# Grouping the U products in pairs, and issuing the repeats of each gated block from two queues

## The chip, the cores and the metric

The kernel runs on one core of a Trainium2 chip. The metric is the device time of one execution in microseconds, as the median of a few runs. The rows of the profile come from one further execution.

## What is computed

For 8 sequences of 1024 tokens with 512 channels in float32, two layers each add to their input. The first is an adapter with weights chosen by a language number. The second uses exponential moving averages over time:

```
x = x + layernorm(x + relu(x W1[lang] + b1) W2[lang] + b2) * gamma0 + beta0
ctx    = ema(x, tau_ctx)
gated  = x * sigmoid([x, ctx] Wg + bg)
mod    = 0.5 + sigmoid(gelu(x Wn1 + bn1) Wn2 + bn2)          # 8 values per token
traces = ema(gated * mod[d], tau[d])  for d = 0..7
temporal = sum over d of traces[d] * softmax(blend)[d]
gate   = sigmoid(temporal Wtemp + btemp)
soma   = gelu(x Wsoma + bsoma)
x = x + layernorm((soma * gate) Wout) * gamma1 + beta1
```

Here ema(b)[t] = alpha * ema(b)[t-1] + b[t].

## The kernel before

The 8192 tokens are cut into 16 tiles of 512, and each tile into 4 blocks of 128 tokens. A tile takes one slot, and the slots follow one another. Five programs run side by side, one for each engine: SyncE (SP) issues nearly all DMAs, ScalarE (ACT) does sigmoid, gelu and the rounded high parts, VectorE (DVE) does the elementwise work, GpSimd (POOL) does some additions, TensorE (PE) the matmuls. Each engine runs its instructions in the order written, and waits on semaphores where a `wait_ge` stands. The orders are written out by hand.

Large products are made of three matmuls each (high times high, high times low, low times high), all 128x128 weights with 512 columns. They write to five PSUM banks used in turn (`ring`), in the order that `groups_of` lists; before a bank is written again PE waits for its reader (`free_bank`).

The part that the change touches is how the eight traces of a block are made. Block b of the gated values, `g[:, b, :]`, is opened by ACT (`open_gate(b)`, a sigmoid), multiplied by DVE (`gated(b)`), and stored by ACT to memory (`store_spans(b)`, 256 KB). It is then read back four times over: `repeat_spans(b)` issues NQ = 4 DMAs of 256 KB, number q of which fills partitions 32q to 32q+31 of a buffer with the whole block, cut in four spans of 32 tokens. Blocks 0 and 2 land in `grep[0]`, block 1 in `grep[1]`, block 3 in the tile's `x1` buffer. All repeats are issued by SP, which waits first for the landing of the store (`g_stored[b]`), then for the buffer to be free.

DVE multiplies a landed block with the blend weights: `products(b, hh, c)` makes one piece of `U` (128x1024), for two halves of the traces (hh) and two halves of the channels (c), four pieces a block. There are four buffers for pieces of U. PE turns each pair of pieces into part of the trace with `within_spans(b, hh)`: matmuls with weights 128x32 and 256 columns that write 32 partitions each. A call of it is 16 matmuls in the profile, 8 for each piece (each float32 matmul appears twice). `from_before(b)` adds what came before the block (3 matmuls, with V, the states of the spans), ACT copies the bank (`trace(b)`), and `trace_by_channels(b)` transposes it for the next tile's gate.

V comes about thus: PE's `span_states()` needs all four gated blocks, DVE scales the result (`span_states()`, L878), ACT rounds it (`states_high()`, L538), DVE takes the low part (`states_low()`, L884). In DVE's order `states_low()` stands between `products(1, 1, 0)` and `products(1, 1, 1)`; `gated(3)` stands ahead of `products(1, 0, 0)`. In ACT's order, ahead of the soma and trace work of the slot:

```
store_spans(0)
for b in range(1, NB):
    open_gate(b)
    store_spans(b)
states_high()
```

Between the `within_spans` PE does the soma products, 12 matmuls each, split in two halves of six (`soma_begun(e)`, `soma_ended(e)`). In tiles with an even number there is also `tile_state()`, three matmuls. After the repeats of a tile SP issues the store of the next tile's x1 and the loads for the tile after it.

Of the kernel before, what the change touches and what calls it, by code (L numbers as in the profile page):

```python
# [11 lines left out]
NB = TOK // P  # L12
NC = C // P
L = 32
NI = P // L
NQ = 4
# [24 lines left out]
def cond_resid_kernel(nc, x, xc, ids, w1, w2, b1, b2, g0, be0, wg, wn1, wsoma, wtemp, wout, wn2,  # L41
# [10 lines left out]
    with ctx:  # L52
# [164 lines left out]
        def upto(per_tile, tile, j):  # L217

            return tile * per_tile + (j + 1)
# [63 lines left out]
        def _(sp):  # L283
# [56 lines left out]
            def slot(k):  # L340
                has_prev, has_cur, has_next = parts_of(k)

                def repeat_spans(b):


                    sp.wait_ge(g_stored[b], 16 * upto(1, k, 0))
                    if b == 2:
                        sp.wait_ge(U_ready, upto(PIECES, k, 3))
                    elif b == 3:
                        sp.wait_ge(g_ready, upto(4, k, b))  # L350
                        sp.wait_ge(x1_stored, 16 * upto(1, k, 0))
                    elif b == 0 and has_next:
                        sp.wait_ge(x1_ready, upto(4, k + 1, NB - 1))
                    for q in range(NQ):
                        sp.dma_start(spans_of(k, b)[q * L:(q + 1) * L, :, :],  # L355
                                     g_dram[b].rearrange("(i s) c -> s i c", i=NI)).then_inc(spans_in(k, b)[0], 16)

                if has_prev:
                    if has_next:
                        if k & 1:  # L360
                            load_language((k + 1) // 2)
                        sp.wait_ge(U_ready, upto(PIECES, k - 1, PIECES // 2 - 1))
                        load_xT(k + 1)
                        sp.wait_ge(U_ready, upto(PIECES, k - 1, 3 * PIECES // 4 - 1))
                        load_x(k + 1)
                        sp.wait_ge(full["h"], upto(1, k + 1, 0))
                    else:
                        sp.wait_ge(U_ready, upto(PIECES, k - 1, PIECES // 2 - 1))
                    sp.dma_start(x1_back[:, :, :].rearrange("p b c -> p (b c)"), x1_dram[(k - 1) & 1]).then_inc(ld_back, 16)
                    for b in range(NB):  # L370
                        sp.wait_ge(res_ready, upto(4, k - 1, b))
                        sp.dma_start(out_tiles[k - 1, b * P:(b + 1) * P, :], res[:, b, :]).then_inc(stored, 16)
                else:
                    second_loads()
                if has_cur:
                    for b in range(NB):
                        repeat_spans(b)
                if has_next:
                    sp.wait_ge(x1_stored, 16 * upto(1, k, 0))
                    keep_x1(k + 1)  # L380
# [71 lines left out]
        def _(act):  # L452
# [6 lines left out]
            def slot(k):  # L459
# [67 lines left out]
                def store_spans(b):  # L527
                    act.wait_ge(g_ready, upto(4, k, b))
                    nc.scalar.dma_start(g_dram[b], g[:, b, :]).then_inc(g_stored[b], 16)

                def open_gate(b):
                    act.wait_ge(pre_ready, upto(4, k, b))
                    nc.scalar.activation(g[:, b, :], g[:, b, :], ACT.Sigmoid).then_inc(sig_ready, 1)  # L533

                def states_high():
                    rows = state_rows(k)
                    act.wait_ge(V_ready, upto(1, k, 0))
                    nc.scalar.activation(V_hi[rows, :], smp[rows, :], ACT.Identity).then_inc(Vhi_ready, 1)  # L538
# [5 lines left out]
                if has_cur:  # L544
                    if k == 0:
                        split(4)
                        split(5)
                    open_gate(0)
                    act.wait_ge(m_pre, upto(1, k, 0))
                    nc.scalar.activation(m_nat, m_nat, ACT.Sigmoid).then_inc(msig_ready, 1)  # L550
                    if k == 0:
                        act.wait_ge(tables_ready, 1)
                        nc.scalar.activation(Epow[0][:, :, :], Epow_raw[:, :, :], ACT.Identity).then_inc(tablehi_ready, 1)
                        nc.scalar.activation(Eend[0][:, :], Eend_raw[:, :], ACT.Identity).then_inc(tablehi_ready, 1)
                    store_spans(0)
                    for b in range(1, NB):
                        open_gate(b)
                        store_spans(b)
                    states_high()
                    soma_gelu(1)  # L560
                    trace(0)
                    trace(1)
                    trace_high(0)
                    soma_gelu(2)
                    trace(2)
                    trace_high(1)
                    trace(3)
                    trace_high(2)
                    if not k & 1:

                        act.wait_ge(full["carry"], k // 2 + 1)
                        nc.scalar.activation(V_hi[96:128, :], smp[96:128, :], ACT.Identity).then_inc(carry_ready, 1)
                    if has_next:
                        soma_gelu(3)
                        trace_high(3)
                    else:
                        trace_high(3)
                        soma_gelu(3)
# [394 lines left out]
        def _(pe):  # L973
# [14 lines left out]
            def slot(k):  # L988
# [37 lines left out]
                def soma_begun(e):  # L1026

                    ps = free_bank(pe, "soma", k, e)
                    at = slice(e * P, (e + 1) * P)
                    split_product(ps[:, :], lambda a, n: Wsoma[a][:, n, at], lambda a, n: x1T[a][:, n, :],  # L1030
                                  NC // 2, final=False)

                def soma_ended(e):

                    at = slice(e * P, (e + 1) * P)
                    split_product(bank_of("soma", k, e)[:, :], lambda a, n: Wsoma[a][:, n, at], lambda a, n: x1T[a][:, n, :],
                                  NC, begin=NC // 2, first=False).then_inc(full["soma"], 1)
# [60 lines left out]
                def value_gate(b):  # L1098

                    ps = free_bank(pe, "wg", k, b)  # L1100
                    at = slice(b * P, (b + 1) * P)
                    split_product(ps[:, :], lambda a, n: x1T[a][:, n, at], lambda a, n: Wg[a][:, n, :], NC, final=False)
                    if b == 0:
                        pe.wait_ge(emalo_ready, upto(4, k, NC - 1))
                        if k == 0:
                            pe.wait_ge(split_lo[3], 1)
                    split_product(ps[:, :], lambda a, n: seq[a][:, n, at], lambda a, n: Wg[a][:, NC + n, :], NC,
                                  first=False).then_inc(full["wg"], 1)
# [77 lines left out]
                if has_cur:  # L1186
                    if k == 0:
                        pe.wait_ge(split_lo[1], 1)
                    soma_of(0)
                    if k == 0:  # L1190
                        pe.wait_ge(split_lo[2], 1)
                    value_gate(0)
                    modulation()
                    value_gate(1)
                    spread_modulation()
                    value_gate(2)
                    value_gate(3)
                    within_spans(0, 0)
                    soma_begun(1)
                    within_spans(0, 1)  # L1200
                    span_states()
                    soma_ended(1)
                    within_spans(1, 0)
                    soma_begun(2)
                    from_before(0)
                    within_spans(1, 1)
                    from_before(1)
                    within_spans(2, 0)
                    trace_by_channels(0)
                    soma_ended(2)  # L1210
                    within_spans(2, 1)
                    from_before(2)
                    soma_begun(3)
                    within_spans(3, 0)
                    trace_by_channels(1)
                    if not odd:
                        tile_state()
                    within_spans(3, 1)
                    from_before(3)
                    trace_by_channels(2)  # L1220
                    if has_next:
                        soma_ended(3)
                        trace_by_channels(3)
                    else:
                        trace_by_channels(3)
                        soma_ended(3)
# [86 lines left out]
```

## Time and profile before

| | |
|---|---|
| three runs | 1365.42, 1373.02, 1372.81 us; median 1372.81 us |
| profiled execution, its own time | 1370.63 us |
| its span, first to last instruction | 1368.8 us |
| mean granted TensorE clock | 0.993 of full speed |
| PE busy | 1326.8 us, 97% of the span |
| DVE, ACT, POOL busy | 1032.8, 522.2, 373.9 us |
| DMA | 186.25 MB, mean 136 GB/s |
| a tile in the steady state | about 82.4 us |

The profiled execution lies 2.2 us under the median of the runs. A busy PE in this profile means that a matmul was in the pipeline, and successive matmuls overlap: a 128x512 matmul lasts 0.39 us and the next one starts 0.23 us after it. What a stretch of PE work costs is therefore read from the starts of the matmuls, not from their durations.

### The profile page before, as it was taken

Reading aid. Unit: us, or ns where it says so; the run is one execution under the profiler, and the core shown is the slowest. Engines: PE = TensorE matmul, PEld = TensorE weight load, DVE = VectorE, ACT = ScalarE, POOL = GpSimd, SP = SyncE. Lnnn points to the kernel's source line nnn. Section 1 sums busy time; section 2 is a strip of 40 time slices with the busy share of each in tenths; the row PEclk is TensorE's granted clock in tenths of the full one; section 3 lists DMA queues with packets and bytes.
Section 4 is the critical chain, followed back from the end, with each engine's and each line's share of the span. In section 5 each row is a group of like instructions: output and inputs, shape, how many; then the busy total and the mean of one; then the engine's idle time right before and its main releaser. Section 6 shows DMA issues by size and latency. Waiting matters only on the chain.

```text
span 1368.8 us, 19735 instructions
## 1 busy us (share of the span) xinstructions
PE 1326.8 (97%) x7908; PEld 982.6 (72%) x7908; DVE 1032.8 (75%) x1526; ACT 522.2 (38%) x822; POOL 373.9 (27%) x294
## 2 busy tenths in 40 slices
PE   4789999999999999999999999999999999999997
PEld 2657768677786767868677686767868677786766
DVE  6997777786778777687786778877777787778575
ACT  3425244252533425244242433425244252433422
POOL 3406123041420504124041322314123041321102
PEclk9899999999999999999999999999999999999999
DMA  7373451916328082461806627074451825426070
GB/s 265 123 205 111 120 180 60 227 69 171 137 85 231 35 227 78 115 204 66 238 32 158 188 78 201 31 215 131 112 166 70 218 90 154 154 77 170 27 190 31
DMA packets 91486, 186.25 MB, mean 136 GB/s; under 512 B 9858, under 2 KB 14594, under 8 KB 87298
## 3 DMA queue, kind: packets, MB, share of 16 engines
q1 hardware_dynamic: 82178, 168.20, 41.8%
q10 hardware_dynamic: 9216, 16.78, 3.7%
q8 instruction: 63, 1.03, 0.3%
q14 instruction: 29, 0.24, 0.1%
HBM read 134.61 MB, written 50.33 MB: 135 GB/s over the span
## 4 chain that ended last, share of the span: by engine, by line
PE 73%; DVE 9%; DMA 6%; issue 5%; ACT 2%; SPq 1%; POOL 1%; DVEq 0%; POOLq 0%
PE ring L984 51%; PE Tp L1158 7%; PE ring L977 4%; PE Tp L1169 3%; DMA grep<-g_blocks 3%; DMA g_blocks<-g_f 3%; PE ring L1183 2%; DVE U L863 2%; PE Tp L984 2%; SPq L355 1%; DVE x L793 1%; PE ring L1004 1%; PE Tp L1004 1%; DVE stats L798 1%; ACT U L523 1%
## 5 line engine op out<-in xcount | busy, mean ns | idle before, releaser
L863 DVE TENSOR_TENSOR U<-grep,w_qs 128x1024 f32<-128x1024 f32 x192 | 227.3, 1218 | 52.9 <-issue 36.1
L412 POOL TENSOR_TENSOR x<-grep,b_row 128x512 f32<-128x512 f32 x64 | 80.0, 1283 | 543.2 <-DMA grep<-in_x 543.2
L1158 PE MATMUL Tp<-U,Arep 128*32 128x256 f32 x2048 | 139.5, 386 | 3.4 <-DVE U L863 3.1
L533 ACT ACTIVATE g_f<-g_f 128x512 f32<-128x512 f32 x64 | 40.4, 632 | 258.2 <-DVE g_f L868 258.1
L425 POOL TENSOR_TENSOR grep<-grep,beta_row 128x512 f32<-128x512 f32 x64 | 82.7, 1326 | 125.3 <-DMA grep<-x_tiles 125.2
L984 PE MATMUL ring<-x1T_hi,Wsoma_hi 128*128 128x512 f32 x256 | 108.3, 423 | 0.0
L868 DVE TENSOR_TENSOR g_f<-ring,bg_row 128x512 f32<-128x512 f32 x64 | 44.1, 689 | 84.8 <-PE ring L984 84.6
L984 PE MATMUL ring<-seq_hi,Wtemp_hi 128*128 128x512 f32 x256 | 106.6, 417 | 0.1
L1158 PEld LDWEIGHTS Tp<-U,Arep 128*32 128x32 f32 x2048 | 51.9, 109 | 74.2 <-issue 38.8
L984 PE MATMUL ring<-Wg_hi,x1T_hi 128*128 128x512 f32 x256 | 103.2, 403 | 0.0
L984 PE MATMUL ring<-Wout_hi,g_r 128*128 128x512 f32 x256 | 99.8, 390 | 1.1 <-DVE soma_r L720 1.0
L984 PE MATMUL ring<-x1T_hi,Wsoma_r 128*128 128x512 f32 x256 | 100.5, 393 | 0.0
L984 PE MATMUL ring<-x1T_lo,Wsoma_hi 128*128 128x512 f32 x256 | 100.1, 391 | 0.0
L984 PE MATMUL ring<-Wg_hi,x1T_lo 128*128 128x512 f32 x256 | 100.1, 391 | 0.0
L984 PE MATMUL ring<-Wg_r,x1T_hi 128*128 128x512 f32 x256 | 99.8, 390 | 0.0
L984 PE MATMUL ring<-seq_hi,Wtemp_r 128*128 128x512 f32 x256 | 99.8, 390 | 0.0
L984 PE MATMUL ring<-seq_lo,Wtemp_hi 128*128 128x512 f32 x256 | 99.7, 390 | 0.0
L984 PE MATMUL ring<-Wout_r,g_r 128*128 128x512 f32 x256 | 99.6, 389 | 0.0
L984 PE MATMUL ring<-Wout_hi,soma_r 128*128 128x512 f32 x256 | 99.6, 389 | 0.0
L984 PE MATMUL ring<-Wg_hi,seq_hi 128*128 128x512 f32 x256 | 99.6, 389 | 0.0
L984 PE MATMUL ring<-Wg_r,seq_hi 128*128 128x512 f32 x256 | 99.6, 389 | 0.0
L984 PE MATMUL ring<-Wg_hi,seq_lo 128*128 128x512 f32 x256 | 99.6, 389 | 0.0
(173 smaller groups left out, 2884.0 us busy)
## 6 DMA issues: line engine op xcount, KB each, us to landing
grep<-g_blocks SPq DMA_DIRECT2D x192, 256.0 KB, 4.5
grep<-in_xc SPq DMA_DIRECT2D x16, 1024.0 KB, 11.3
grep<-in_x SPq DMA_DIRECT2D x16, 1024.0 KB, 9.0
x_tiles<-x SPq DMA_DIRECT2D x16, 1024.0 KB, 9.0
g_blocks<-g_f ACTq DMA_DIRECT2D x64, 256.0 KB, 3.7
x<-g_blocks SPq DMA_DIRECT2D x64, 256.0 KB, 5.7
grep<-x_tiles SPq DMA_DIRECT2D x16, 1024.0 KB, 4.8
out<-U SPq DMA_DIRECT2D x64, 256.0 KB, 2.0
```

What stands on the lines that cost most here:

```text
L355: sp.dma_start(spans_of(k, b)[q * L:(q + 1) * L, :, :], g_dram[b].rearrange("(i s) c -> s i c", i=NI)).then_inc(spans_in(k, b)[0], 16)
L412: nc.gpsimd.tensor_tensor(new[:, b, :], x_t[:, b, :], b2_row[:, :], ALU.add).then_inc(xb2_ready, 1)
L425: nc.gpsimd.tensor_tensor(x1_back[:, b, :], x1_back[:, b, :], beta1_row[:, :], ALU.add).then_inc(x1b_ready, 1)
L533: nc.scalar.activation(g[:, b, :], g[:, b, :], ACT.Sigmoid).then_inc(sig_ready, 1)
L863: V_.tensor_tensor(U[:, (n + 2) % 4, :, :], spans_of(k, b)[:, :, at], w_qs[:, hh, at].unsqueeze(1).to_broadcast([P, NI, HC]), ALU.mult).th ...
L868: V_.tensor_tensor(g[:, b, :], bank_of("wg", k, b)[:, :], bg_row[:, :], ALU.add).then_inc(pre_ready, 1)
L977: last = nc.tensor.matmul(dst, lhsT(n), rhs(n), start=(n == 0), stop=(n == steps - 1))
L984: last = nc.tensor.matmul(dst, lhsT(a, n), rhs(b, n), start=(first and n == begin and m == 0), stop=(final and n == steps - 1 and m == 2))
L1004: last = nc.tensor.transpose(ps[:, b * P:(b + 1) * P], x1[odd ^ 1][:, b, n * P:(n + 1) * P], ident[:, :])
L1158: last = nc.tensor.matmul(Tp[b % 2][i * L:(i + 1) * L, at], Arep[:, b * NI + i, hh, :], U[:, (n + 2) % 4, i, :], start=(hh == 0 and c == 0 ...
L1169: last = nc.tensor.matmul(Tp[b % 2][:, :], Epow[a][rows, b, :], V[c][rows, :], start=False, stop=(m == 2))
L1183: last = nc.tensor.transpose(ps[:, n * P:(n + 1) * P], T_sb[b % 2][:, n * P:(n + 1) * P], ident[:, :])
```

## The change

Two things change. First, SP issues only the repeats with q = 0 and 1 of each block, and ACT issues those with q = 2 and 3, right behind the store of the block, with a wait for the landing of that store and the same waits for a free buffer. Second, PE's order is changed so that the two `within_spans` of a block follow one another, with the soma products moved out from between them.

```
@@ SP
-                    for q in range(NQ):
+                    for q in range(NQ // 2):
@@ ACT
+                def repeat_spans(b):
+                    act.wait_ge(g_stored[b], 16 * upto(1, k, 0))
+                    if b == 0 and has_next:
+                        act.wait_ge(x1_ready, upto(4, k + 1, NB - 1))
+                    elif b == 1 and has_prev:
+                        act.wait_ge(res_ready, upto(4, k - 1, NB - 1))
+                    elif b == 2:
+                        act.wait_ge(U_ready, upto(PIECES, k, 3))
+                    elif b == 3:
+                        act.wait_ge(x1_stored, 16 * upto(1, k, 0))
+                    for q in range(NQ // 2, NQ):
+                        nc.scalar.dma_start(spans_of(k, b)[q * L:(q + 1) * L, :, :],
+                                            g_dram[b].rearrange("(i s) c -> s i c", i=NI)).then_inc(spans_in(k, b)[0], 16)
...
                     store_spans(0)
+                    repeat_spans(0)
                     for b in range(1, NB):
                         open_gate(b)
                         store_spans(b)
+                        repeat_spans(b)
                     states_high()
@@ PE
+                    soma_begun(1)
                     within_spans(0, 0)
-                    soma_begun(1)
                     within_spans(0, 1)
                     span_states()
                     soma_ended(1)
+                    soma_begun(2)
                     within_spans(1, 0)
-                    soma_begun(2)
+                    within_spans(1, 1)
                     from_before(0)
-                    within_spans(1, 1)
                     from_before(1)
+                    soma_ended(2)
+                    trace_by_channels(0)
                     within_spans(2, 0)
-                    trace_by_channels(0)
-                    soma_ended(2)
                     within_spans(2, 1)
                     from_before(2)
                     soma_begun(3)
+                    trace_by_channels(1)
                     within_spans(3, 0)
-                    trace_by_channels(1)
+                    within_spans(3, 1)
+                    from_before(3)
                     if not odd:
                         tile_state()
-                    within_spans(3, 1)
-                    from_before(3)
                     trace_by_channels(2)
```

## Rows read from the trace of the kernel before

**Rows 1.** The page, part 1: busy time, share of the span, instructions.
```profile
PE 1326.8 (97%) x7908; PEld 982.6 (72%) x7908; DVE 1032.8 (75%) x1526; ACT 522.2 (38%) x822; POOL 373.9 (27%) x294
```

**Rows 2.** Waits of the span: total us, times, longest us.
```profile
DVE U L863 <- DMA grep<-g_blocks: 16.7, 15, 1.8
```

**Rows 3.** Chain that ended last, one odd tile: start us, us, what.
```profile
482.14 2.61 DMA g_blocks<-g_f
...
484.76 0.33 SPq L355
...
494.71 3.99 DMA g_blocks<-g_f
...
498.72 0.30 SPq L355
...
500.02 6.68 DMA grep<-g_blocks
```

**Rows 4.** Timeline of ACT, the same tile: start us, us, what, [idle before].
```profile
487.56 0.33 ACTq L529 DMA_DIRECT2D g_blocks<-g_f  x1
...
497.64 0.63 ACT L533 ACTIVATE g_f<-g_f 128x512 f32<-128x512 f32 x1 [4.03 <-DVE g_f L868]
499.03 0.36 ACTq L529 DMA_DIRECT2D g_blocks<-g_f  x1
502.14 0.60 ACT L538 ACTIVATE V_hi_r<-smp 120x512 fp32r<-120x512 f32 x1 [3.87 <-DVE smp L878]
```

**Rows 5.** Stores issued at 487.56 and 577.70: KB, us to landing.
```profile
g_blocks<-g_f ACTq DMA_DIRECT2D x1, 256.0 KB, 4.0
...
g_blocks<-g_f ACTq DMA_DIRECT2D x1, 256.0 KB, 3.8
```

**Rows 6.** Timeline of DVE, the same odd tile.
```profile
498.31 0.69 DVE L872 TENSOR_TENSOR g_f<-g_f,x 128x512 f32<-128x512 f32 x1 [0.70 <-ACT g_f L533]
...
503.15 0.68 DVE L884 TENSOR_TENSOR V_lo_r<-smp,V_hi_r 120x512 fp32r<-120x512 f32 x1
503.75 1.22 DVE L863 TENSOR_TENSOR U<-grep,w_qs 128x1024 f32<-128x1024 f32 x1
506.73 4.63 DVE L863 TENSOR_TENSOR U<-grep,w_qs 128x1024 f32<-128x1024 f32 x4 [1.76 <-DMA grep<-g_blocks]
```

**Rows 7.** Timeline of PE, the same odd tile.
```profile
505.59 0.39 PE L1169 MATMUL Tp<-V_lo_r,Epow_hi 128*128 128x512 f32 x1
505.82 0.40 PE L1169 MATMUL Tp<-V_hi_r,Epow_r 128*128 128x512 f32 x1
506.14 1.07 PE L1158 MATMUL Tp<-U,Arep 128*32 128x256 f32 x16
507.14 0.50 PE L1169 MATMUL Tp<-V_hi_r,Epow_hi 128*128 128x512 f32 x1
...
508.10 0.64 PE L1158 MATMUL Tp<-U,Arep 128*32 128x256 f32 x8
...
517.54 0.50 PE L1169 MATMUL Tp<-V_hi_r,Epow_hi 128*128 128x512 f32 x1
...
518.36 0.60 PE L1183 MATMUL ring<-ident,T_sb_f 128*128 128x128 f32 x4
518.71 0.48 PE L984 MATMUL ring<-x1T_hi,Wsoma_hi 128*128 128x512 f32 x1
```

**Rows 8.** Timelines of ACT and of PE in the next tile, an even one.
```profile
577.70 0.33 ACTq L529 DMA_DIRECT2D g_blocks<-g_f  x1
...
598.32 0.47 PE L1176 MATMUL smp<-V_hi_r,Eend_hi 128*128 128x512 f32 x1
...
600.19 0.50 PE L1169 MATMUL Tp<-V_hi_r,Epow_hi 120*128 120x512 f32 x1
```

**Rows 9.** DMA rate in 40 slices of 491.5 to 498.8, and of 511 to 523.
```profile
GB/s 0 0 0 0 0 79 146 11 180 325 449 359 292 224 213 191 213 202 213 157 258 348 269 225 225 202 224 202 213 202 213 213 247 314 314 202 56 0 0 0
...
GB/s 437 410 369 348 403 396 416 403 403 416 410 314 396 416 382 403 396 410 396 430 266 157 34 0 0 0 0 0 0 0 0 0 0 0 0 0 0 0 0 0
```

## The prediction

> **What bounds the kernel now.** I read the page first. PE is busy 97% of the span [rows 1], so a gain has to come either from PE work made cheaper or from the few places where PE waits. Next I read the waits. DVE waits once per tile, about 1.1 us, for the repeats of block 2 (16.7 us over 15 tiles) [rows 2]. The chain of waits over one odd tile shows why: a store of a gated block lands about 4 us after its issue, SP then issues four repeats, and the last of them lands at 506.70 [rows 3]. Last I read the timelines of DVE, PE and ACT for that tile [rows 4, 6, 7]. DVE begins block 2 at 506.73, the moment the repeat is there, and PE's last groups of the tile follow DVE's pieces closely. So in this stage PE's own work, DVE's pieces and the repeats are all nearly critical, and a delay of over a microsecond in any of them reaches the end. The rest of the slot (gates, output, soma) is dense PE work. Therefore I measure a tile by one mark, the start of `from_before(3)`, which is 517.54 in the odd tile and 600.19 in the next, even one [rows 7, 8]. What follows the mark stays the same but for one step, counted below.
>
> **Part 1, the pairing on PE.** A lone `within_spans` starts 0.32 after the matmul before it, where a 128x128 one starts 0.23 after: 0.09 more. The next wide matmul starts 1.00 after the group's start, and the one after that later than usual by 0.13, since three matmuls and their successor take 0.82 where 0.23 each would give 0.69 [rows 7]. One piece alone lasts 0.64 and two last 1.07, so a piece adds 0.43, and a second group behind the first should cost 0.86 instead of 1.00 [rows 7]. I take the same cadence of 0.43 across the border of the groups, which no row shows; the lone price is its upper bound. A pairing then saves 0.09 + 0.13 + 0.14 = 0.36 us, four of them in 16 tiles 23 us. This is a gain only if PE is what decides. Moving `tile_state` behind the mark adds three matmuls there in even tiles, 3 x 0.23 = 0.7 us.
>
> **Part 2, two repeats leave SP.** SP's four issues begin 1.30 apart from first to last, 0.43 each [rows 3]. With two per queue the last begins 0.35 to 0.45 after the first. At most 0.95 us is saved on each block, at least nothing, because the transfer itself is the longer piece: after a short burst the rate stays at 190 to 230 GB/s for the whole of a block's repeats, while the loads to 128 partitions run at about 400 [rows 9]. I take 0.2 us per block, near the lower end, since four requests already queue behind each other. SP itself gains 0.9 us per block, worth nothing: nobody waits for what follows.
>
> **Part 3, ACT now waits.** This is the part that decides. ACT runs in order, and its new wait for the landing of store b stands ahead of `open_gate(b+1)` and, for b = 3, ahead of `states_high()`. Blocks 0 and 1 do no harm: store 0 lands at 484.75 [rows 3], ACT has issued its pair at 485.6, and with a sigmoid and a product still between, store 1 left only at 487.56 [rows 4]. Followed through the odd tile:
> - Store 2 is issued at 494.71 and lands at 498.7 [rows 3]. Two issues take 0.8, so ACT is free at 499.5. Its sigmoid of block 3 started at 497.64 [rows 4]; it is 1.9 late.
> - From that sigmoid to DVE's `gated(3)` is 0.67, from there to store 3 is 0.72 [rows 4, 6]: store 3 goes out at 500.9, not 499.03. DVE stands still meanwhile, as `products(1, 0, 0)` is behind `gated(3)`, and PE's `span_states` stands too.
> - Store 3 lands in the traffic of block 2's repeats, begun at 498.7. The nearest case is store 1, issued 2.8 after block 0's repeats began (484.76) and landed 4.0 later, 6.8 after their begin [rows 3 to 5]. I take 6.8: 505.5. The bounds are 3.8 after its issue, 504.7 [rows 5], and the end of block 2's traffic as it was, 8.0 after its begin, 506.7 [rows 3].
> - ACT issues its pair (0.8) and only then rounds V (0.6), 506.9 instead of 502.7. DVE's `states_low` takes 0.6 and `products(1, 1, 1)` 1.2 [rows 4, 6]: its piece is ready at 508.7 instead of 504.97, 3.7 us late.
> - PE reaches this piece at about 506, so it waits. Block 2 has landed by then, so the old wait of DVE is gone. From here on, with t the time of that piece: half a group 0.57, twelve matmuls 0.82 + 9 x 0.23 = 2.9, four transposes 0.35 and the entry 0.09 give t + 3.9 for block 2's groups; 1.86 for the pair, nine matmuls 2.2, transposes and entry 0.44 give t + 8.4 for block 3's; its last piece is reached at t + 9.7. DVE needs 4.63 + 0.6 + 4.63 = 9.9 for the eight pieces and one low part [rows 6], so PE gets it at t + 9.8, and the mark is at t + 10.4 [rows 7].
>
> **The sum.** Odd tile: 508.7 + 10.4 = 519.1 against 517.54, 1.6 us late. Even tile: store 2 goes out at 577.70 and lands 3.8 later, 581.5 [rows 5, 8]; store 3 goes out at 583.7 and lands at 588.3; the piece is ready at 591.5, the mark at 601.9 against 600.19: 1.7 us, and 0.7 for `tile_state`. The mean is 2.0 us. The drains of blocks 1 and 2 both lie on this path, so 0.2 us saved on each takes off 0.4, leaving 1.6 us a tile and 26 us for 16 tiles. Against the profiled execution's own 1370.6 us this is 1397; the median of the runs stands 2.2 us above, so I predict **1399 us**. With the bounds of the landing (-0.8 and +1.2 a tile) the case spans 1386 to 1418.
>
> The Trainium skill, "DMA: Bandwidth & Descriptors", section "Issuing engines are not separate DMA queues", says that DMAs begun on several engines run on the same sixteen engines and save only the sequencer's time. By that rule the sum stays at 26 to 32 us, less at most the issue time bounded above.
>
> **Rival A, two queues fill two halves at once: faster.** SP now fills partitions 0 to 63 and ACT 64 to 127 together, where one queue filled them in turn. For it: 200 GB/s against 400 for full-width loads, and a bump to 348 GB/s in the middle of block 1's repeats, where the third repeat takes over from the second [rows 9]. Against it: both queues feed the same engines, and the burst at the start appears with a single queue too. At 400 GB/s 1 MB takes 2.6 us instead of 5.1. Then block 1 is in before store 2 goes out, and store 2 lands in 2.6 as store 0 did [rows 3], at 497.3; store 3 goes out at 499.5 and lands after some 3.2 (between 2.6 and 3.8), 502.7; the piece is ready at 505.9, the mark at 516.3. That is 1.2 us earlier in odd tiles, 0.4 in even ones (1.1 less 0.7), 13 us in all: 1360 us. It decides once the two drains together are more than 2.0 us shorter, 1.0 of 6.8 us each.
>
> The skill's "SBUF — State Buffer", section "Door 1: The DMA port swizzle", puts partitions 0 to 63 on one half of the ports and 64 to 127 on the other, which is this rival's mechanism. The same page reports that two concurrent transfers to the two halves gained only 6%, which speaks for the forecast; no run so far shows either.
>
> **Rival B, the two effects cancel.** The drains get about 1.0 us shorter each, by part overlap plus the issue time. The delay of 2.0 us a tile is then paid back: 1373 us.
>
> **Rival C, the pairing pays in full.** ACT's waits hide and PE alone decides: 23 us less, 1350 us. Against it: the piece behind `states_low` cannot come before ACT has issued its second pair.
>
> **Chances.** Forecast 0.55, rival A 0.22, rival B 0.18, rival C 0.05. Differences under 1% cannot be told from none here, so faster means under 1359 and slower above 1387. A sits on the first border, so I give half of it and all of C to faster, and a little more: 0.18. B, the rest of A and the forecast's low tail make 0.29 for same, and 0.53 is left for slower. The range reaches from below A, 1354, to 1412 within the forecast's upper tail.
>
> **What would show it.** Right: ACT's sigmoid of block 3 near 2 us later than before, measured from the last gate product; `states_high` 4 us later; a new wait of PE for U in the second group of block 1; no wait of DVE for block 2's repeat; the DMA rate still near 200 GB/s. Wrong: the rate near 400 during the repeats, stores landing in under 3 us, or the mark earlier than before. The pairs themselves are right if two groups start 0.86 apart.

## The result and the profile after

| kernel | median us | lowest, highest | profiled execution, its span | mean granted clock |
|---|---|---|---|---|
| before | 1372.91 | 1365.42, 1373.9 | 1370.63, 1368.8 | 0.993 |
| after | 1399.59 | 1395.73, 1406.9 | 1406.9, 1405.1 | 0.984 |

The change makes the kernel slower: ratio 1.0207, 95% interval 1.0172 to 1.0241. The profiled execution of the changed kernel is the slowest of its four, 7.3 us above the median. So its trace shows some 36 us of loss where the median shows 27. One execution of experiment 1's kernel below, 2846.97 us at full clock, is left out of its ratio as slow.

The page of the kernel after, part 1, and its views of waits (total us, times, longest us). They answer to [rows 1, 2].

```profile
PE 1326.9 (94%) x7908; PEld 1004.1 (71%) x7908; DVE 1036.7 (74%) x1526; ACT 521.2 (37%) x822; POOL 375.2 (27%) x294
...
ACT V_hi_r L552 <- DMA g_blocks<-g_f: 88.8, 15, 7.1
...
PEld Tp L1174 <- DVE U L879: 50.8, 36, 3.7
...
ACT g_f L547 <- DMA g_blocks<-g_f: 41.7, 7, 6.2
...
DVE V_lo_r L900 <- ACT V_hi_r L552: 27.5, 16, 3.0
```

PE has the same work as before (1326.9 us busy), in a longer span. DVE's wait for the repeats of block 2 is gone. In its place ACT waits for the landing of its own stores, ahead of V's rounding and ahead of the sigmoid; DVE waits for the rounded V; PE waits for DVE's pieces, its weight loads up to 3.7 us at once and its matmuls up to 3.2.

The chain of waits through the same odd tile as in [rows 3], start us, us, what:

```profile
502.09 3.46 DMA g_blocks<-g_f
505.55 0.02 issue
505.57 0.36 ACTq L542
505.93 0.03 issue
505.96 0.46 ACTq L542
506.42 0.05 issue
506.46 0.64 ACT g_f L547
...
507.12 0.70 DVE g_f L888
...
507.85 5.41 DMA g_blocks<-g_f
...
514.16 0.61 ACT V_hi_r L552
...
515.39 1.23 DVE U L879
516.62 0.04 issue
516.66 1.08 PE Tp L1174 x8
```

This is the forecast's path, link by link: store 2, ACT's two issues, the late sigmoid of block 3, store 3, ACT's two issues, the rounding of V, the piece behind `states_low`, and PE. Before the change the chain of this stretch ran over SP and the repeats instead. PE in the same tile; these rows answer to [rows 7]:

```profile
506.28 1.93 PE L1174 MATMUL Tp<-U,Arep 128*32 128x256 f32 x32
508.03 1.04 PE L1156 MATMUL smp<-g_f,Bm 128*32 128x512 f32 x8
...
511.95 1.50 PE L1174 MATMUL Tp<-U,Arep 128*32 128x256 f32 x24
516.66 1.08 PE L1174 MATMUL Tp<-U,Arep 128*32 128x256 f32 x8 [3.21 <-DVE U L879]
...
518.27 0.63 PE L1185 MATMUL Tp<-V_lo_r,Epow_hi 128*128 128x512 f32 x1
518.69 0.63 PE L1185 MATMUL Tp<-V_hi_r,Epow_r 128*128 128x512 f32 x1
...
528.59 0.50 PE L1185 MATMUL Tp<-V_hi_r,Epow_hi 128*128 128x512 f32 x1
```

Three things are to be seen. The pair takes 508.03 - 506.28 = 1.75 us up to the next group, so the pairing works as costed. PE stands 3.21 us for the last piece of block 1. And behind that wait the same matmuls are slow: a piece takes 1.08 instead of 0.64, and matmuls follow each other in 0.42 instead of 0.23. The reason is the clock. The rows below are stretches of 1 us of this tile. The columns are the length, the busy us of PE, PE's weight loads, DVE, ACT and POOL with their instructions, the granted clock, the DMA share and GB/s:

```profile
513.00:514.00 1.00, 0.45 (x11) 0.00 (x0) 0.00 (x0) 0.00 (x0) 0.00 (x0) 1.00 0.00 0
514.00:515.00 1.00, 0.00 (x0) 0.00 (x0) 0.21 (x1) 0.82 (x2) 0.00 (x0) 1.00 0.90 100
515.00:516.00 1.00, 0.00 (x0) 0.00 (x0) 1.00 (x2) 1.00 (x1) 0.00 (x0) 1.00 0.49 176
516.00:517.00 1.00, 0.34 (x4) 0.20 (x8) 1.00 (x2) 0.74 (x2) 0.00 (x0) 0.64 1.04 330
517.00:518.00 1.00, 1.00 (x9) 0.33 (x2) 1.00 (x2) 0.00 (x0) 0.00 (x0) 0.50 1.06 254
518.00:519.00 1.00, 1.00 (x3) 0.81 (x3) 1.00 (x2) 0.00 (x0) 0.00 (x0) 0.50 1.10 361
519.00:520.00 1.00, 1.00 (x4) 0.76 (x4) 1.00 (x2) 0.60 (x1) 0.00 (x0) 0.66 1.01 426
520.00:521.00 1.00, 1.00 (x6) 0.79 (x5) 1.00 (x2) 0.60 (x1) 0.00 (x0) 1.00 0.99 418
```

Near the end of PE's standstill of 3.2 us the granted clock falls from 1.00 to 0.50, the lower level of 1.2 GHz, and it comes back near 519.7. The piece and the six matmuls behind it take 3.4 us from start to start; at full clock they take 0.57 + 0.34 + 5 x 0.23 = 2.1.

The length of a wait alone does not tell whether the clock falls, and a fall can begin after PE has resumed. After the first 100 us the changed kernel's PE waits more than 1.5 us at fifteen places, and at eight of them the clock falls. The waits at these eight last 1.57 to 3.21 us, those at the other seven 1.57 to 1.97. In experiment 2 below, three waits of 2.4 to 2.5 us pass with the clock at 1.00. One place of each kind, first of the kernel after, then of experiment 2's (PE with its wait, then a stretch of 2 us behind it, columns as above):

```profile
180.35 0.64 PE L1174 MATMUL Tp<-U,Arep 128*32 128x256 f32 x8 [1.86 <-DVE U L879]
```

```profile
182.00:184.00 2.00, 2.00 (x6) 1.52 (x6) 2.00 (x3) 1.11 (x2) 0.00 (x0) 0.50 1.06 407
```

```profile
264.88 0.64 PE L1160 MATMUL Tp<-U,Arep 128*32 128x256 f32 x8 [2.43 <-DVE U L865]
```

```profile
264.00:266.00 2.00, 1.12 (x10) 0.64 (x11) 2.00 (x3) 0.95 (x2) 0.00 (x0) 1.00 1.02 264
```

To compare kernels I use two numbers. The first is the mean over 16 tiles of the forecast's mark: the start of `from_before(3)`, counted from the start of the last `value_gate` matmul of the tile. The second is the clock loss: (1 - granted clock) times length, summed over stretches of 2 us from 100 us on, without the last microseconds of the span, where the clock falls in every kernel. It is an upper figure, as some of that time PE is idle anyway. For before they are 21.20 and 0.0 us, for after 22.89 and 15.4 us. Their first tiles aside, the marks of the changed kernel spread from 20.2 to 25.7 us, those of before from 20.4 to 21.6.

### The profile page after: what moved, and what is told of

It reads as the page before. It is cut to its first block, busy times and chain, and to the rows that moved or that the text cites. A ratio compares the mean times of both kernels' runs of the same rounds, so it can differ in the third digit from the quotient of the medians.

```text
span 1405.1 us, 19797 instructions
## 1 busy us (share of the span) xinstructions
PE 1326.9 (94%) x7908; PEld 1004.1 (71%) x7908; DVE 1036.7 (74%) x1526; ACT 521.2 (37%) x822; POOL 375.2 (27%) x294
## 4 chain that ended last, share of the span: by engine, by line
PE 65%; DVE 12%; DMA 10%; issue 4%; ACT 3%; ACTq 2%; POOL 1%; DVEq 0%; POOLq 0%
PE ring L1000 45%; DMA g_blocks<-g_f 9%; PE Tp L1174 5%; PE Tp L1185 4%; DVE U L879 4%; PE ring L993 3%; PE Tp L1000 2%; PE ring L1199 2%; ACTq L542 2%; DVE g_f L888 2%; DMA grep<-g_blocks 1%; PE Tp L1020 1%; PE ring L1020 1%; ACT g_f L547 1%; DVE g_f L884 1%
## 5 line engine op out<-in xcount | busy, mean ns | idle before, releaser
L1174 PE MATMUL Tp<-U,Arep 128*32 128x256 f32 x2048 | 131.3, 386 | 34.3 <-DVE U L879 34.3
L425 POOL TENSOR_TENSOR grep<-grep,beta_row 128x512 f32<-128x512 f32 x64 | 87.0, 1391 | 146.1 <-DMA grep<-x_tiles 146.1
L1174 PEld LDWEIGHTS Tp<-U,Arep 128*32 128x32 f32 x2048 | 56.4, 109 | 94.3 <-DVE U L879 50.8
```

The source lines that it names most:

```text
L425: nc.gpsimd.tensor_tensor(x1_back[:, b, :], x1_back[:, b, :], beta1_row[:, :], ALU.add).then_inc(x1b_ready, 1)
L1174: last = nc.tensor.matmul(Tp[b % 2][i * L:(i + 1) * L, at], Arep[:, b * NI + i, hh, :], U[:, (n + 2) % 4, i, :], start=(hh == 0 and c == 0 ...
```

## The experiments

All ratios are against the kernel before, timed on the same chip. The experiments were timed on three chips, on which the kernel before took 1371.5 to 1372.5 us; the changed kernel was timed beside one of 1372.9 us. So differences in microseconds between kernels are good to a few us only. "Paired" means PE's new order.

**1. The pairing alone (pair_only).** The changed kernel's PE order, with SP and ACT as before. Seen from the changed kernel:

```
-                    for q in range(NQ // 2):
+                    for q in range(NQ):
-                        repeat_spans(b)          # and repeat_spans(0), on ACT
```

> PE's new order alone; SP issues all four repeats as before and ACT waits for nothing new. Theory (ACT's in-order wait for the landing of its stores is what costs): DVE keeps its old pace, the mark of a tile moves 0.5 us forward at most and tile_state takes 0.7 us back in even tiles, so 0 to 8 us faster than before, ratio 0.994 to 1.000. Rival (the pairing itself costs, as PE meets U pieces too early and then stands): at least 15 us slower, ratio 1.01 or more.

Measured: 1361.71 us, ratio 0.9933 (0.9907 to 0.996). Mean mark 20.56, clock loss 3.4 us. The rival falls: the pairing pays, a bit more than the theory gave it. Full payment would have been 23 us. DVE's pieces most likely take the rest, as PE still waits for them (profile of this kernel, waits):

```profile
PEld Tp L1158 <- DVE U L863: 37.1, 56, 2.1
DVE U L863 <- DMA grep<-g_blocks: 12.7, 13, 2.6
```

**2. ACT's waits alone (wait_only).** As 1, and ACT waits where the change waits, but issues no repeats:

```
                     store_spans(0)
+                    act.wait_ge(g_stored[0], 16 * upto(1, k, 0))
                     for b in range(1, NB):
                         open_gate(b)
                         store_spans(b)
+                        act.wait_ge(g_stored[b], 16 * upto(1, k, 0))
```

> PE's new order, SP issues all four repeats, ACT issues none but waits for the landing of each store at the place where the change waits. Theory: the wait alone brings the loss back, ACT being 0.8 us freer per block but the transfer longer: ratio 1.010 to 1.025, PE waiting for U in the second group of block 1. Rival (not the wait but two queues sharing the DMA engines cost): same as the pairing alone, ratio within 0.003 of it.

Measured: 1415.18 us, ratio 1.0341 (1.0273 to 1.0409). Against experiment 1 the waits alone cost 53 us, 3.3 us a tile. The direction is the theory's, the size was outside its range. Mean mark 23.62, clock loss 17.1 us. No DMA was moved, so the two queues are not the culprit. Since the changed kernel has the same waits, and its two issues of 0.4 us behind each of them besides, and is still 16 us faster, its split must even help.

**3. The split with ACT's waits, PE in its old order (split_only).** The changed kernel with the PE order of before.

> The repeats from two queues with ACT's waits, PE in its old order. Theory: the late piece behind states_low is as late as in the changed kernel, and PE then takes the lone groups, each 0.36 us dearer: ratio 1.020 to 1.030. Rival (the pairing costs): ratio below 1.005, since two queues land a block about 0.8 us sooner.

Measured: 1386.24 us, ratio 1.0135 (1.0079 to 1.0192). Slower as the theory said, but less than it said: the new PE order does not soften the loss. By the medians it adds to it, though the two intervals overlap slightly (up to 1.0192 here, from 1.0172 in the changed kernel). The clock loss is 0.0 us here.

**4. ACT's waits with the old PE order (wait_old).** The kernel before with only the two `wait_ge` of experiment 2. It asks by a second pair of kernels what the pairing costs when a piece is late.

> The kernel before, with only ACT's waits for the landing of each store added; PE in its old order, all repeats from SP. Theory (with a late piece the pairing collects PE's idle time in one place, and costs instead of paying): PE still does from_before(0) in the shadow of the late piece and its gaps stay under 2 us, ratio 1.015 to 1.026, well under the 1.034 of the same waits with the pairing. Rival (pairing saves its 0.36 us per block whatever the rest does): ratio 1.040 or more.

Measured: 1397.23 us, ratio 1.0191 (1.0144 to 1.0237), as the theory said; the rival falls. With the same waits the pairing costs 18 us more (1415.18), and without them it saves 10. Clock loss 0.0 here, 17.1 with the pairing; the mean granted clock is 0.992 against 0.980. PE's waits behind the late V in this kernel:

```profile
PEld Tp L1171 <- DVE V_lo_r L886: 24.3, 15, 2.2
PE Tp L1171 <- DVE V_lo_r L886: 19.0, 15, 1.7
PEld Tp L1160 <- DVE U L865: 16.4, 42, 1.5
```

They are cut in two: first for V's low part ahead of `from_before(0)`, then for U, with work between. In the paired order the two fall into one (waits of wait_only):

```profile
PEld Tp L1160 <- DVE U L865: 55.7, 35, 3.8
PE Tp L1160 <- DVE U L865: 39.7, 21, 3.3
```

**5. Work moved into the gap (filled).** The changed kernel with one move on PE:

```
                     soma_begun(2)
+                    soma_begun(3)
                     within_spans(1, 0)
                     within_spans(1, 1)
...
                     from_before(2)
-                    soma_begun(3)
```

> The changed kernel with soma_begun(3) moved ahead of within_spans(1, 0), so that 1.4 us of work that PE does later stand in front of its long wait. The late piece comes no sooner. Theory (part of the loss is the granted clock, which falls to half after PE's gap of 3 us and more in some tiles): the gap shrinks by 1.4 us, the clock stays up, and PE catches up with DVE's pieces: 8 to 18 us faster than the changed kernel, ratio 1.008 to 1.015. Rival (only DVE's pieces decide behind the wait): within 4 us of the changed kernel, ratio 1.018 to 1.024.

Measured: 1390.44 us, ratio 1.0159 (1.0111 to 1.0208). That is 9 us under the changed kernel's median, just outside the ratio that the theory named, and its interval overlaps the changed kernel's. The time alone does not settle it. In the trace the clock loss falls from 15.4 to 5.1 us, and in the tile looked at PE waits 1.63 us and then runs a piece in 0.64 (PE of this kernel, [idle before]):

```profile
508.31 0.64 PE L1174 MATMUL Tp<-U,Arep 128*32 128x256 f32 x8 [1.63 <-DVE U L879]
508.88 0.50 PE L1185 MATMUL Tp<-V_hi_r,Epow_hi 128*128 128x512 f32 x1
509.22 0.39 PE L1185 MATMUL Tp<-V_lo_r,Epow_hi 128*128 128x512 f32 x1
```

Nor does this run part the clock from a plainer cause: the move also fills 1.4 us in which PE would have stood still, and that could shorten the tile by itself. By the ratios the gain is 7 us.

**6. Both of ACT's harmful waits moved back (split_late).** The changed kernel, in ACT's order (written here several calls to a line):

```
-                    for b in range(1, NB):       # open_gate(b), store_spans(b), repeat_spans(b)
+                    open_gate(1); store_spans(1); repeat_spans(1)
+                    open_gate(2); store_spans(2)
+                    open_gate(3); repeat_spans(2)
+                    store_spans(3)
                     states_high()
+                    repeat_spans(3)
```

> As the changed kernel, but ACT begins its repeats of block 2 behind the sigmoid of block 3, and those of block 3 behind states_high; PE's new order and both queues stay. Theory: ACT's waits now stand behind what others need, and block 2 lands 0.8 us sooner than before: ratio 0.985 to 0.997. Rival (the two queues or the pairing cost): stays at 1.015 or more.

Measured: 1359.68 us, ratio 0.9913 (0.9887 to 0.994), within the theory's range. Mean mark 20.16, clock loss 0.0. Both parts of the change are still in it, so neither the split nor the pairing is what costs; the place of ACT's waits is.

**7. Only block 3's pair behind the rounding of V (late_states).** The changed kernel with `repeat_spans(3)` moved behind `states_high()`.

> The changed kernel with one move: ACT's repeats of block 3 stand behind states_high. Theory: V is rounded at once and the piece behind states_low is held back only by the late gate of block 3, 1.9 us; about 2 us a tile come back: ratio 0.995 to 1.005. Rival (the late gate of block 3 is what decides, and V is only late because of it): no more than 0.5 us a tile comes back, ratio 1.015 or more.

Measured: 1365.31 us, ratio 0.9946 (0.9927 to 0.9965), just under the theory's range. One instruction group moved past another gives back 34 us of the changed kernel's median. Mean mark 20.38, clock loss 0.0.

**8. Only block 2's pair behind the sigmoid of block 3 (late_gate).** The changed kernel with `open_gate(3)` ahead of `repeat_spans(2)`; block 3's pair stays ahead of `states_high()`.

> The changed kernel with the other move: ACT's repeats of block 2 stand behind the sigmoid of block 3, those of block 3 still ahead of states_high. Theory: store 3 leaves about 1 us sooner, V is still held back until it lands: about 1 us a tile comes back, ratio 1.005 to 1.014. Rival (the late gate decides): near the pairing alone, 0.993 to 1.000.

Measured: 1418.14 us, ratio 1.0327 (1.0294 to 1.0359). A miss: not a microsecond came back, 19 us were lost. The chain of this kernel, same columns as above:

```profile
512.67 0.64 ACT g_f L547
...
513.33 0.70 DVE g_f L893
...
514.05 5.29 DMA g_blocks<-g_f
...
520.24 0.60 ACT V_hi_r L552
```

The sigmoid is on time, but store 3, now issued amid block 2's repeats, takes longer to land: 5.4 us in the median of the tiles against 4.1 in the changed kernel. What ends V's wait is the drain of the traffic around the store, not the moment of its issue. The traces show it over all 16 tiles (medians): store 3 leaves 1.1 us after block 2's first repeat here and 2.3 us after it in the changed kernel, block 2 takes 5.9 us from first issue to last landing in both, and in both store 3 lands 0.5 us after the last of these repeats. So V is rounded 8.8 us after the last `value_gate` matmul here and 8.9 us there: the earlier store bought nothing. The 19 us have another source. PE gets to its wait sooner, as the gate is on time, and stands there longer: its matmuls wait 47.5 us in all for pieces of U against 34.3, and the clock loss is 28.8 us, the largest of the study, against 15.4. That the clock makes up most of the 19 us fits these numbers, but no run tested it by itself.

**9. Both queues on the same half (same_half).** The changed kernel with SP issuing q = 0, 2 and ACT q = 1, 3:

```
-                    for q in range(NQ // 2):             # SP
+                    for q in (0, 2):
-                    for q in range(NQ // 2, NQ):         # ACT
+                    for q in (1, 3):
```

> The changed kernel, but SP issues the repeats 0 and 2 and ACT 1 and 3, so that both queues fill partitions 0 to 63 first and 64 to 127 then. Theory A (the higher rate in the changed kernel's repeats comes from filling both halves of the partitions at once): the rate falls back to about 200 to 230 GB/s, a block lands about 0.8 us later, and the kernel is 0.5 to 1% slower than the changed one, ratio 1.026 to 1.036. Rival (two queues do it, whatever they fill): like the changed kernel, ratio 1.017 to 1.024.

Measured: 1448.54 us, ratio 1.054 (1.0501 to 1.0579). Theory A's direction, over three times its size. Mean mark 25.70, clock loss 27.3 us. The same queues, bytes and waits; only which partitions are filled together differs. DMA rates in 40 slices while block 0 is repeated, first the kernel after (492.8 to 498.6), then this one (508.4 to 515.2):

```profile
GB/s 0 0 0 0 0 0 0 56 28 113 155 282 367 381 410 410 410 410 382 424 353 282 240 282 226 212 240 226 381 325 424 339 226 226 282 339 381 184 42 0
```

```profile
GB/s 0 0 0 0 0 12 108 108 96 217 289 386 410 361 253 229 217 193 205 205 193 217 229 325 217 205 217 241 217 217 205 205 193 205 193 253 361 349 145 36
```

After: over a microsecond at 350 to 424 GB/s, and a second, shorter rise. Same half: a short burst that reaches 410 as well, then about 205, which is the picture of before [rows 9]. From the first issue of block 0's repeats to DVE's first product of it this tile takes 6.4 us before (484.76 to 491.12), 5.6 after and 6.7 here. Over all tiles, the median from the first issue of a block's repeats to the last landing, blocks 0 to 3, is 6.6, 6.5, 7.1 and 7.8 us before, 5.5, 6.2, 5.9 and 6.4 after, and 6.6, 6.9, 6.6 and 7.2 here. Per DMA, from issue to landing (part 6 of the pages, after and then same_half):

```profile
grep<-g_blocks SPq DMA_DIRECT2D x96, 256.0 KB, 4.1
grep<-g_blocks ACTq DMA_DIRECT2D x96, 256.0 KB, 4.7
```

```profile
grep<-g_blocks SPq DMA_DIRECT2D x96, 256.0 KB, 4.8
grep<-g_blocks ACTq DMA_DIRECT2D x96, 256.0 KB, 5.6
```

**10. One queue, the halves in turn (pair_alternate).** As 1, all repeats from SP:

```
-                    for q in range(NQ):
+                    for q in (0, 2, 1, 3):
```

> The pairing alone, all four repeats from SP, in the order 0, 2, 1, 3 instead of 0, 1, 2, 3. Theory A (halves of the partitions decide): three borders between halves instead of one, a block lands 0.2 to 0.5 us sooner, ratio 0.988 to 0.993. Rival (one queue is worked off in order and gains nothing): equal to the pairing alone, 0.993, with the same time to landing.

Measured: 1358.0 us, ratio 0.9883 (0.9847 to 0.992). The interval overlaps that of experiment 1 a little, but the traces side with theory A: the median landing of a repeat to `grep` falls by 0.5 us (part 6 of the pages, experiment 1 and then this kernel),

```profile
grep<-g_blocks SPq DMA_DIRECT2D x192, 256.0 KB, 4.5
```

```profile
grep<-g_blocks SPq DMA_DIRECT2D x192, 256.0 KB, 4.0
```

and DVE's wait for repeats from 12.7 us to 2.6. From first issue to last landing block 0 takes 6.2 us instead of 6.5 (medians), within the 0.2 to 0.5 us of the theory. The rate no longer settles at 205; 40 slices of 481.4 to 487.4, block 0 of this kernel:

```profile
GB/s 0 0 0 0 0 0 96 177 191 164 287 369 355 287 314 341 410 287 301 219 232 218 341 314 164 164 177 300 287 410 342 300 246 219 314 423 232 218 41 0
```

Mean mark 19.96. This is the lowest median of the study, 1.1% under the kernel before and 41 us under the changed one, with no second queue at all. Its interval overlaps that of experiment 6.

**11. The same order of repeats in the kernel before (old_alternate).**

> The kernel before with one edit: SP issues the repeats in the order 0, 2, 1, 3. Theory (PE's lone groups are the floor in the old order, DVE only just behind them): marks fall to the 20.4 us that the best tiles of the old order have, 0.6 us a tile, ratio 0.992 to 0.996. Rival (the transfer of block 2 decides the old order's tiles): 1 us a tile or more, ratio 0.988 or less.

Measured: 1369.47 us, ratio 0.9982 (0.996 to 1.0004). No change that can be told, though DVE's wait for repeats to `grep` fell from 16.7 to 2.7 us. Without the pairing PE's lone groups are the floor, and quicker repeats have little to give. That was the theory's reason, but its size was too hopeful: its floor of 20.4 us left out `tile_state()`. The marks are now 20.39 us in most odd tiles and 21.08 in most even ones, which have these three matmuls ahead of the mark, so the mean fell only from 21.20 to 21.04.

The ratios side by side:

| how the repeats are begun | PE's old order | paired |
|---|---|---|
| SP, in order | 1 | 0.9933 |
| SP, ACT only waits | 1.0191 | 1.0341 |
| SP and ACT, as the change has it | 1.0135 | 1.0207 |
| SP, halves in turn | 0.9982 | 0.9883 |
| SP and ACT, ACT's waits moved back | not run | 0.9913 |

## Why the prediction was right, and where it was right by luck

The direction and its cause are shown. ACT's in-order wait costs 53 us by itself (experiment 2 against 1) and moving it gives the loss back (6 and 7). The predicted 1399 us and the measured 1399.6 agree better than the terms deserve: the loss from pairing and ACT's part was put at less than half, the gain from the filling of both halves at an eighth, and the clock was missing. Here is each step, by the tile that the forecast followed, from the start of its last `value_gate` matmul (496.49 before, 504.60 after):

- *The pairing.* Predicted 0.86 us for the second group; 1.75 us for two up to the next group against 0.89 for one gives 0.86. Right. As a saving it was worth 10 us alone, not 23, most likely because DVE's pieces follow closely: PE still waits for them in experiment 1.
- *The late sigmoid of block 3.* Predicted 1.9 us late; it starts at +1.86 instead of +1.15, so 0.7. Too large. Store 2 left 0.7 earlier and landed in 3.46 instead of 3.99 us, most likely because the repeats of blocks 0 and 1 landed sooner.
- *The landing of store 3.* Predicted 6.8 us after block 2's repeats began; 7.7 here (505.57 to 513.26), inside the bounds. The median of the tiles is 6.4.
- *The rounding of V and the piece.* Predicted 4.2 and 3.7 us late; +9.56 against +5.65 is 3.9, and the piece, ready at 516.6, is 3.5 late. Right in size, as the two errors before it cancel.
- *From the piece to the mark.* Predicted 10.4 us, measured 528.59 - 516.62 = 12.0. This is the missing term: the granted clock at 0.50 for about 3 us, which makes 1.3 to 1.4 of the 1.6 us (3.4 instead of 2.1 from the piece through six matmuls). The forecast had PE waiting some 2.7 us there and never asked what a stand of that length does to the clock.
- *What the split saves.* Predicted 0.2 us per block; 0.8 us on block 0 of this tile (6.4 to 5.6), and 1.1, 0.3, 1.2 and 1.4 us for blocks 0 to 3 by the medians of experiment 9. Some of the gain of blocks 2 and 3 is not the split's: with ACT's waits alone (experiment 2) block 2 already takes 6.5 us. Mis-sized: the forecast took the number nearest to "bound by the transfer", and gave the filling of both halves only a rival's chance. That rival's mechanism is real, in part.

By medians of whole kernels the pairing gave -10 us (1371.5 to 1361.7), ACT's waits +53 (to 1415.2) and the split -16 (to 1399.6). That is +28 against the kernel before of those runs, and +27 against the 1372.9 beside which the changed kernel was timed. These steps do not match the forecast's terms one for one. Its +32 us for pairing and ACT's part contain ACT's two issues of 0.8 us ahead of the sigmoid and ahead of the rounding, 1.6 us a tile or 26 us, which experiment 2 does not have.

The kernel that has all that the +32 us stand for, with transfers as slow as the forecast took them, is experiment 9. There block 0 takes 6.6 us to land, as before, and the kernel is 76 us slower (1448.5 against 1372.5). V is rounded 5.5 us later than before on the mean of the tiles, where the forecast followed 4.2, the mark comes 4.5 us later, and up to 27 us of the loss is clock. From there to the changed kernel the filling of both halves takes 49 us off, where the forecast had -6 for the split. So +32 stood for up to +76 and -6 for up to -49, and that the total came out at 26 against 27 is luck. How much of the 76 us belongs to two queues working on one half, a case that the forecast did not have, is open; block 1 takes 6.9 us there against 6.5 before.

Of the signs that the prediction named, four of the right ones came: `states_high` 3.9 us later in this tile, PE's new wait for U in block 1, no wait of DVE for block 2's repeat, and two groups 0.86 apart. Two did not: the sigmoid was 0.7 us late instead of near 2, and the rate did not stay near 200 GB/s. Two of the signs of being wrong came as well: rates near 400 during the repeats, and a store landing in under 3 us (block 1's, median 2.7). They belong to the misjudged split.

On rival A: its mechanism is shown by experiments 9 and 10, which change nothing but which partitions are filled together. Its sum failed because the drains of blocks 1 and 2 would have had to be 1.0 us shorter each, and they were 0.3 and 1.2 us shorter (medians), and because it too left out the clock. The Trainium skill, "SBUF — State Buffer", section "Door 1: The DMA port swizzle", puts partitions 0 to 63 and 64 to 127 on different ports; the order of the rates here agrees (same half about 205 GB/s after the burst, both halves 350 to 424 for over a microsecond). The same page, section "Can I just issue two DMAs to hit both halves?", reports only 6% for two concurrent transfers to the two halves. Here the block came 0.8 of 6.4 us sooner, over 12%, of which up to 0.95 us could also be issue time; but experiment 10, with one queue and the same number of issues, also shortened the landing by 0.5 of 4.5 us, and that cannot be issue time. On this the measurement decides, for this pattern of 2 KB runs to 32 partitions.

Rival B's amount did not come about, rival C's neither: its reason to fail, the piece behind `states_low`, is what the chain shows.

Still open: why the marks of the changed kernel scatter from 20.2 to 25.7 us from tile to tile, what decides which of PE's waits the clock falls at, and how much of the summed clock loss lay on the path.

## What to carry to other kernels

Before a DMA is moved to a compute engine's queue, write down what stands behind it in that engine's order: the issue costs 0.4 us, but the wait in front of it held up the next sigmoid and the rounding of V, and moving one group behind another turned 2% slower into 0.5% faster. Where several small DMAs fill parts of the partitions, try their order first; 0, 2, 1, 3 instead of 0, 1, 2, 3 gave at least as much as the second queue did with its waits in a harmless place. And grouping PE's work pays only as long as nothing in the group is late: it also groups PE's waits, and at about half of the waits of 1.5 to 3.2 us in the changed kernel the clock fell to half.

## What the runs showed of the hardware

- Repeats to 32 partitions each settled at about 205 GB/s, after a short burst, as long as queued neighbours filled the same half of the partitions. With both halves filled from two queues the rate stayed at 350 to 424 GB/s for over a microsecond; from one queue in the order 0, 2, 1, 3 it swung between 164 and 423.
- The granted clock fell from 1.00 to 0.50 near the end of a standstill of PE of 3.2 us, and stayed there for about 3 us of dense work. In experiment 4, whose longest wait of this kind was 1.7 us, it did not fall before the last microseconds. In the changed kernel it fell at waits from 1.57 us on, while experiment 2 had waits of 2.4 to 2.5 us without a fall. The Trainium skill, "TensorE: Matmul & The Clock Gate", section "Part 1: The HAM clock gate", names two states, 1.2 GHz when idle and 2.4 GHz when busy; the trace agrees with the two levels, 0.50 and 1.00.
- A 256 KB store issued 1 us or more after a block's repeats had begun landed with the last of them. In experiments 2, 4 and 8 store 3 took 5.4 us (medians), and it landed 0.2, 0.2 and 0.5 us after block 2's last repeat, whether the repeats came from SP alone or from SP and ACT. In the kernel before it left 0.4 us after the first repeat, took 3.8 us and landed 3.1 us ahead of the last one. Store 0, with no repeats around it, took 2.1 us (median).
